# Earlier squares in the main loop, and a reordered end, in a wave-sampling attention and expert kernel

## The reference

```python
h = _layernorm(x) * (1 + ca) + sa
x = x + ga * silu(attention(h) @ out_w.T)
h = _layernorm(x) * (1 + cb) + sb
mask = one_hot(top_k(softmax(h @ router_w.T + router_b), 2)).sum(-2)
x = x + gb * (einsum('bse,ehd,bsd->bsh', mask, expert_w, h) + mask @ expert_b)
```

## Time and profile before

| quantity | value |
|---|---|
| median of 3 runs | 293.26 us |
| lowest and highest of them | 291.19 and 295.67 us |
| profiled execution, device time | 293.6 us |
| profiled execution, span of the trace | 291.8 us |
| granted TensorE clock, mean | 0.998 |
| busy share of PE, DVE, ACT, POOL | 90%, 90%, 78%, 21% |

### The profile page before, as it was taken

One profiled execution on the slowest core, in us unless ns is written; L12 is line 12 of the kernel. 1 busy time (PEld: TensorE's weight loads), 2 busy tenths in 40 slices (PEclk: granted clock), 3 DMA queues, 4 the chain that ended last, 5 costly groups with the idle time before them and its releaser, 6 DMA issues.

```text
span 291.8 us, 5429 instructions
## 1 busy us (share of the span) xinstructions
PE 262.0 (90%) x1867; PEld 181.0 (62%) x1876; DVE 262.0 (90%) x543; ACT 226.9 (78%) x641; POOL 62.7 (21%) x59
## 2 busy tenths in 40 slices
PE   8899886899798999889998999889999989899995
PEld 3544642665486487647784569548884768476664
DVE  7989989998979999999999899989999999982671
ACT  4885899699897998699869989799779767655310
POOL 4103101800451023502080026202340300010100
PEclk9999999999999999999999999999999999999999
DMA  6560000020004000320014000500041004100101
GB/s 179 161 160 0 0 0 0 3 74 1 1 2 163 2 1 0 97 86 3 0 29 155 0 0 2 183 2 1 2 130 53 1 0 125 60 2 0 36 2 54
DMA packets 12011, 12.93 MB, mean 44 GB/s; under 512 B 1021, under 2 KB 10960, under 8 KB 11216
## 3 DMA queue, kind: packets, MB, share of 16 engines
q1 hardware_dynamic: 11540, 12.19, 13.9%
q10 hardware_dynamic: 444, 0.40, 0.5%
HBM read 10.44 MB, written 2.15 MB: 43 GB/s over the span
## 4 chain that ended last, share of the span: by engine, by line
ACT 31%; PE 26%; DVE 18%; POOL 12%; issue 11%; ACTq 0%; DVEq 0%; POOLq 0%
PE pE L1136 9%; ACT A L507 8%; DVE AT L835 8%; POOL rs L327 8%; ACT xn L405 4%; ACT c L490 4%; POOL nm L329 4%; PE pE L985 3%; ACT xn L371 3%; DVE T L802 3%; PE pY L1136 3%; PE pR L1028 2%; ACT hT L428 2%; ACT y L529 2%; DVE hm L902 2%
## 5 line engine op out<-in xcount | busy, mean ns | idle before, releaser
L802 DVE COPY_PREDICATED T<-mask,T 128x1472 f32<-128x1472 int16 (+9 forms) x54 | 76.2, 1411 | 0.5
L835 DVE TENSOR_TENSOR AT<-T,c 128x2064 f32<-128x2064 f32 x32 | 72.3, 2300 | 0.0
L1136 PE MATMUL pE<-hm,late 128*128 128x256 f32 x224 | 52.6, 386 | 0.0
L1136 PEld LDWEIGHTS pE<-hm,late 128*128 128x128 f32 x224 | 41.2, 190 | 6.6
L507 ACT ACTIVATE A<-pT 128x512 f32<-128x512 f32 x64 | 34.7, 600 | 12.6 <-PE pT L1051 12.5
L327 POOL TENSOR_TENSOR rs<-ve,mhalf 128x4 f32<-128x4 f32 (+1 forms) x18 | 32.5, 1806 | 44.3 <-DVE ve L715 37.5
L321 POOL TENSOR_SCALAR ve<-sq 128x4 f32<-128x4 f32 (+1 forms) x14 | 7.0, 502 | 162.9 <-ACT xn L371 162.9
L405 ACT ACTIVATE xn<-x,nm,rs 128x128 f32<-128x128 f32 x64 | 26.5, 485 | 16.1 <-POOL nm L329 16.1
L1051 PE MATMUL pT<-first,AT 128*128 128x128 f32 x256 | 34.2, 276 | 4.8 <-DVE AT L845 4.7
L1051 PEld LDWEIGHTS pT<-first,AT 128*128 128x128 f32 x256 | 28.3, 141 | 11.4 <-DVE AT L845 9.9
L507 ACT ACTIVATE A<-pR 128x512 f32<-128x512 f32 x64 | 35.2, 619 | 0.0
(11 more groups left out here) (145 smaller groups left out, 389.2 us busy)
## 6 DMA issues: line engine op xcount, KB each, us to landing
mkb<-mask_rows SPq DMA_DIRECT2D x6, 1024.0 KB, 5.3
x<-in_x SPq DMA_DIRECT2D x7, 256.0 KB, 6.1
out<-x SPq DMA_DIRECT2D x7, 256.0 KB, 5.3
late<-in_late SPq DMA_DIRECT2D x1, 592.0 KB, 3.9
mkb<-mask_rows SPq DMA_DIRECT2D x1, 512.0 KB, 3.6
x<-in_x SPq DMA_DIRECT2D x2, 128.0 KB, 3.7
wmod<-in_wmod ACTq DMA_DIRECT2D x1, 256.0 KB, 3.5
out<-x SPq DMA_DIRECT2D x2, 128.0 KB, 3.2
```

What stands on the lines that cost most here:

```text
L802: nc.vector.copy_predicated(rows[:, :, :, j0:j1], spread(mask[:, k, 0:w, j0:j1], [P, w, H, j1 - j0], 2), rows[:, :, :, j0 + (1 << bit):j1 ...
L835: nc.vector.tensor_tensor(cells_of(bt).rearrange("p h (j r) -> p h j r", r=BLK), spread(T[n % 2][:, bt, 0:H, 0:NB], [P, H, NB, BLK], 3), s ...
L1136: ins = mm(dst, weT[:, e, :], hm[b][:, e, :], start=False, stop=(e == E - 1))
```

## The change

There are three edits. First, in ScalarE's loop `squares1` of unit i+2 stands ahead of `back_h2T` and `back_moe` instead of behind them. Second, on VectorE at the end, `masked(LATE - 1, 1)` moves behind `residual(LATE)` and `stats2(LATE)`, and a wait for GpSimd's `rs` of unit 7 is put ahead of it. Third, in TensorE's list at the end, 5 and 6 products of zeros are put around `mid_y(LATE)`, the transpose `mid_gate(LATE)` comes after 2 experts of the first image of unit 6 instead of after all 8, and the experts of the second image are cut in other pieces, the last of them behind `back_mk(LATE)`.

```diff
@@ ScalarE, main loop
                 run(i, -1, norm2)
                 if i < 0:
                     run(i, 1, front_hs)
+                run(i, 2, squares1)
                 run(i, -1, back_h2T)
                 run(i, -2, back_moe)
-                run(i, 2, squares1)
                 run(i, 0, mid_A, 0)
@@ VectorE, end
             set_ends(LAST, 0)
-            masked(LATE - 1, 1)
             residual(LATE)
             stats2(LATE)
+
+            dve.wait_ge(g_rs2, LATE + 1)
+            masked(LATE - 1, 1)
             route(LATE)
@@ TensorE, end
             mid_attend(LATE, 1, 1)
+
+            warm_up(5, pT[0])
             mid_y(LATE)
-            back_experts(LATE - 1, 0)
+            warm_up(6, pT[0])
+            back_experts(LATE - 1, 0, range(0, 2))
             mid_gate(LATE)
+            back_experts(LATE - 1, 0, range(2, E))
             mid_A(LAST, 0, 0)
             mid_A(LAST, 0, 1)
             mid_attend(LAST, 0, 0)
             mid_attend(LAST, 0, 1)
-            back_experts(LATE - 1, 1, range(0, 3))
+            back_experts(LATE - 1, 1, range(0, 1))
             back_x2T(LATE)
-            back_experts(LATE - 1, 1, range(3, 4))
             mid_y(LAST)
+            back_experts(LATE - 1, 1, range(1, 3))
             back_logits(LATE)
             mid_gate(LAST)
-            back_experts(LATE - 1, 1, range(4, E))
+            back_experts(LATE - 1, 1, range(3, 6))
             back_mk(LATE)
+            back_experts(LATE - 1, 1, range(6, E))
             back_mb(LATE, 0)
```

## The result

| quantity | before | after |
|---|---|---|
| median, 10 runs each | 292.73 us | 294.63 us |
| lowest to highest | 290.19 to 295.67 | 294.04 to 295.9 |
| profiled execution: device time, span | 293.6, 291.8 | 294.68, 292.9 |
| granted TensorE clock of that execution | 0.998 | 0.988 |

The ratio is 1.0086 (95% interval 1.006 to 1.0113): slower, where 291.4 us and a small gain were forecast. The ratios in this document are the recorded ones with their intervals; they aren't the quotients of the medians beside them, which here is 1.0065. So the changed kernel is between nothing and 1% slower, and in neither set is it faster. The measured time lies outside the forecast range.

The account below looks back on a forecast made before the run. The prediction took a circle through ScalarE, GpSimd and VectorE to bound the loop. From the profiled 293.6 us, -1.3 (loop) and -0.6 (end) gave 291.7, or 291.4 in the median's terms; range 289.4 to 293.9.

Parts of the forecast that it names:

- The loop's circle through GpSimd: Loop: GpSimd's small operations stall behind VectorE's two-input ones, giving the 31.77 us period; squares first saves 1.3 in all.
- The series of lg: Loop, VectorE's lg: its shift against before, +0.55 at i=2, then +1.0, +0.34, -0.3, and -1.3 at i=6.
- signs that the prediction names for the loop: Profile after: rs about 1.1 us, norm1 without wait, residual's 1.0 waits gone, lg waiting 0.3 to 0.5 in iterations 3 to 5.
- TensorE's clock: End: zeros could buy only clock, already 1.00 in that stretch, so nothing; for the loop no clock effect was named.
- 1.0 us of the later h2T: Loop: squares ahead of h2T make h2T, the logits and lg 1.0 us later, counted from the copies to A.
- the 0.1 to 0.2 of late output: End: the experts' new pieces, two behind mk where TensorE waits anyway, put unit 6's output 0.1 to 0.2 us later.
- The shift of unit 8's transposes: End, TensorE: the added zeros make unit 8's transposes come later by 0.2 to 0.7 us, taken as 0.5.
- the first rival: End: nm is caught behind masked, so statistics first gains nothing; 292.2 us, chance 0.25.
- as they should be: Shared-port rule, whichever operation starts first holding the ports throughout: said to fit GpSimd's times of 6.00 and 2.23 us.
- the term of 0.8 us: End: norm2 of unit 7 gains 1.31 us from earlier statistics, less 0.5 for later copies of unit 8.
- The sum: Whole kernel: -1.3 from the loop and -0.6 from the end, 293.6 to 291.7 us, or 291.4 in the median's terms.
- The slower rival: Loop: GpSimd misses the 2.8 us gap between AT pairs, iterations 1 to 5 each pay 1.0; 298.3 us, chance 0.05.

Follow-up runs that it names:

- e5_fill: e1_squares with more zeros in TensorE's loop waits (27 for 18 in iteration 1, 8 for 4 before the logits from iteration 1 on): 0.9918, 291.51 us.
- neither set: The two comparisons of the changed kernel with the kernel before: the first at ratio 1.0086, the repeat (e9_again) at 1.0012.
- second set: Second of three sets of experiment runs, with its own chip and 18 runs of the kernel before, median 293.54 us.
- e1_squares: Kernel before with only ScalarE's squares moved ahead of h2T, the end unchanged: 0.9995, 293.39 us.
- e7_nm: e2_stats with VectorE waiting for nm of unit 7 instead of rs ahead of masked: ratio 1.0 to the kernel before.
- e12_order: e5_fill and e7_nm together, with unit 7's x2T transposes ahead of the second image's experts, one of them before mid_y: 0.9927, 291.6 us.
- e10_after_fill: The changed kernel with the added zeros of e5_fill in TensorE's loop waits, its end as changed: 0.9969.
- e3_pe_end: Kernel before with only TensorE's list at the end changed (zeros and new expert pieces): 1.0042, 294.5 us.
- e9_again: The changed kernel run once more, unchanged, beside its variants on their chip: 1.0012 to the kernel before, 294.06 us.
- e2_stats: Kernel before with only VectorE's residual and statistics of unit 7 moved ahead of masked, with the wait for rs: 0.9996.
- e6_keep1: Kernel before with the squares ahead of h2T in all iterations but iteration 1, where they stay behind; no zeros added: 0.994, 292.03 us.

## Why the prediction was wrong, point by point

- **The loop's circle through GpSimd**: right. rs takes 1.01 instead of 6.00 us, norm1 has no wait in the steady iterations, the period is 30.98 against the 31.1 of the forecast. The series of lg was +0.55, +1.0, +0.34, -0.3, -1.3; after has +1.20, +1.48, +0.68, -0.11, -1.23, e5_fill with its full clock +0.25, +0.53, -0.28, -1.08, -2.02. The term was too small by 0.7 us: with the clock kept, the loop brings 2.0. Nearly all signs that the prediction names for the loop came (the one miss is a wait of 0.64 us for the logits in iteration 3, where 0.3 to 0.5 was said), and none of them could show the clock.
- **TensorE's clock**: the step that failed. The prediction puts it at nothing, in edit 1 without a word and in edit 3 because it is 1.00 in the earlier trace rows; it took 0.95 us in the loop of after (logits of unit 1 at 83.13 against e5_fill's 82.18; 0.79 of it is left at iteration 6) and 1.6 at its end. In edit 1 I priced the 1.0 us of the later h2T on ScalarE and VectorE alone, and let TensorE's longer wait in front of the logits cost nothing. In iteration 1 it is 1.02 us behind one of 2.20, and the clock is at half for 3.4 or 6.8 us: 2.3 us in e1_squares (84.45 against 82.18). The row that I did read, a clock of 1.00, was of other stretches, and of a kernel in which that wait isn't. In the text on edit 3 I say that zeros could buy nothing but clock; I didn't ask it of edit 1.
- **Edit 3, TensorE's end**: I wrote that two experts behind mk stand where TensorE waits anyway. I missed that ScalarE's copy of mkT waits for those very experts, `t_moe` in `back_mk`: 0.8 us, against the 0.1 to 0.2 of late output in the sum. The shift of unit 8's transposes was well sized: forecast 0.5, measured 0.4 (in after they start 0.65 us behind the start of the edge copy, 256.20 and 255.55, and 0.25 before, 257.06 and 256.81).
- **Edit 2, statistics first**: the first rival came. I took it that nm gets in ahead of masked; masked is 0.05 us ahead and nm takes 2.31. The Trainium skill, SBUF — State Buffer, section "SBUF: two separate sides", says that the one that starts first has the shared ports for the whole instruction, and this row of after agrees; which one starts first is what I had wrong. The rows of before are less simple than "as they should be": the rs of 6.00 starts 0.34 us ahead of the AT pair at 178.30 (a VectorE operation with two inputs was running from 177.79), and the rs at 52.37, which was first, did not hold up the pair that began at 53.05; all 32 AT multiplications of before take 2.30 us. There the measurement decides: VectorE isn't seen to wait. Beyond it the term of 0.8 us was wrong: e7_nm had norm2 1.4 us early and gained nothing, and e12_order shows that TensorE's own work bounds that part. In the order of edit 3 TensorE does wait 0.61 us for norm2 (263.50 in after); whether the wait for nm would give that back wasn't run.
- **The sum**: forecast -1.9. In the profile of after: -1.23 from the loop with its fall of the clock in it, another -0.12 up to the logits of unit 7, and +2.43 from there to the logits of unit 8, of which 0.8 is the wait for `t_moe` and 1.6 the fall near 272; +1.08 at the end. That the loop's -1.23 is so near the forecast -1.3 is luck: with the clock kept it brings 2.02 (e5_fill), and after is 0.79 behind that at iteration 6 for its fall near 50. The end was put at -0.6 and shows +2.3; of these 2.9 us the fall near 272, put at nothing, is 1.6, edit 2, which gave next to nothing, 0.7, and the wait for `t_moe` 0.6.
- **The slower rival** ended on the right side for a wrong reason: GpSimd didn't miss the gap.

e5_fill is the version to keep: 0.9918 of before, and with the second set's 291.51 us well under both kernels.

What stays open: why the clock fell near 272 in the profile of after and in e10_after_fill's, by its groups in 7 of 12 runs, but not in e3_pe_end's or e9_again's profile, with the same work in front of it; what makes a fall near 50 come behind the old wait alone in two profiles of five; and why the kernel before had runs of 290.2 to 291.4 us beside the changed kernel and none under 293.2 beside the experiments.

## What to carry to other kernels

When an edit makes an engine wait longer somewhere, look at what TensorE does there as well: a microsecond of new idle time behind an older one can cost its clock, and more than the edit brings; a few products of zeros in both waits gave it back. One profile with a clock of 1.00 doesn't show a wait to be harmless: look at the mean clocks of all runs. Before moving work past a point in one engine's list, read the waits of every instruction that overwrites what that work reads. And an event that lets two engines go at the same time is no order between them: wait for the later result.

## What the runs showed of the hardware

- TensorE went to half rate, 1.2 GHz, in a kernel that keeps it 90% busy, with no idle time longer than 2.20 us near it. After 2.20 us idle alone this came in some executions and not in others (e2_stats and e7_nm against before, e3_pe_end and e6_keep1). With 1.3 us of work and 1.02 us idle behind that, all four profiles have it, and 10 of 11 runs of e1_squares have a mean clock of 0.988 or lower; in e9_again it began ahead of the second of the two waits.
- Each fall in the working part of these profiles lasted 3.4 or 6.8 us.
- The same fall costs more or less by what waits behind it: 3.4 us near 50 cost nothing in e2_stats and e7_nm, 0.95 us in after; 3.4 us near 272 cost 1.6; 6.8 us near 50 cost 2.3 in e1_squares. In the kernel before most runs with a mean clock of 0.994 take the 293.3 us of those with 1.000; a few take 294.0 to 295.5.
- VectorE, released by the end of a GpSimd operation, starts its next one 0.03 us later (258.31 + 1.01 = 259.32 to 259.35), before GpSimd's own next one (0.08 us, 259.40).
